# A cross-attention and FFN kernel: row maxima of two banks in one instruction, their transposes first in attention, additions ahead of low parts

## The chip, the cores and the metric

The kernel runs on one core of a Trainium2 chip. The metric is the time of one execution on the device, in microseconds (us), as the median of several runs. Five engines run their own instruction lists in order and meet at semaphores: TensorE (PE, with its weight loads as PEld), VectorE (DVE), ScalarE (ACT), GpSimd (POOL) and SyncE (SP), which issues nearly all DMAs.

## The reference, cut to what matters

```
x   [4, 2048, 512], ctx [4, 154, 512], 16 heads of 32, 8 key/value heads
q1,q2 = split(LN(x) @ Wq.T)   k1,k2 = split(ctx @ Wk.T)   v = ctx @ Wv.T
attn  = (softmax(q1 k1^T) - lam * softmax(q2 k2^T)) v        # per head, 154 keys
x     = x + (rmsnorm(attn) * g * (1 - 0.8 + 0.6 exp(-3.6))) @ Wo.T
h     = gelu(LN(x) @ ternary(w1).T + b1)                     # 2048 wide
x     = x + LN(h) @ ternary(w2).T + b2
```

All in float32. Both softmaxes subtract the maximum of each row of scores.

## The kernel before, in words

The 8192 rows of x are cut into 16 blocks of 512 rows (NBLK), each block into four tiles of 128 (TT). Products are made from float16 parts: a tensor is split into a high part (ScalarE casts or scales) and a low part (VectorE subtracts), and TensorE multiplies high with high, high with low and low with high.

**Row maxima.** For each of the 4 x 32 rows of scores (4 tiles, 32 units: two softmaxes of 16 heads) the maximum is needed before attention. `row_scores` writes the scores of one tile and three units (two in the last group) into a PSUM bank, 462 numbers a partition, and `row_max` on VectorE reduces that bank to three numbers. There are 44 such banks' worth to a block (NT). They are made for block i+1 inside the FFN loop of block i, MAXIMA_AT[j] of them beside step j. From block 2 on they rotate over four banks: PSUM banks 6, 7, 0, 1; blocks 0 and 1 have two. When all are there, `split_maxima` makes float16 parts of the negated maxima (step TLAST of the loop), TensorE transposes them (`transpose_maxima`, token c), VectorE copies the result (`copy_maxima`, last in its loop), and SP stores it as two further rows of the stacked queries by DMA. The first scores of the next attention wait for that DMA.

**Attention** of a block follows the list ATTEND, which every engine walks, each taking the tokens that concern it:
- s0 to s7: TensorE's scores (4 units a time, L1518 and L1523), ScalarE's exponentials and high parts (L807 to L812), VectorE's low parts (L1127).
- v0 to v7: TensorE's product with the values (L1541 to L1548) and VectorE's normalise; at odd numbers also the difference of both softmaxes and the statistics (L1136 to L1150).
- q0 to q3: queries of the next block (L1430 to L1432), ScalarE's q_hi, GpSimd's q_lo.
- t0 to t2: high and low part of a pair of heads (ScalarE, and VectorE L1155), then SP transposes them by DMA into `rows`, for the output projection behind v7. A fourth comes behind the list. SP issues twelve DMAs of the next block's stacked queries behind t0.
- e1 to e3, h1 to h4: what is left of the FFN of the block before: its second product for tile 1 (e), 2 and 3 (h), in steps of hidden groups given by LATE (L1599). Each step is two matmuls.
- g: TensorE's sums of gelu and its square (L1620), VectorE's gelu_norm, on GpSimd the constant's additions (L672) and a power.
- y0 to y3: VectorE's addition of the FFN's product to x_res (`add_ffn`, L1247), which frees the PSUM bank. Scores 1 wait for y0 and y1, the queries q1 for y2, q2 for y3.
- z0 to z3: VectorE's last addition (`add_shift`, L1256), SP's store and the load of x for the next block.

Behind the list come the output projection (pairs 0 to 2 of all tiles, then pair 3; it goes through L1430 to L1432 as well), the second layer norm and the transposes of its rows.

**The FFN loop** has 16 steps (JH): TensorE's first product (`hidden`, L1583), row scores (L1486), the second product for tile 0 of three steps before (`ffn_step`, L1609); ScalarE's gelu, high part and square; VectorE's maxima (L1105) and gelu low part (L1221), and in steps 7 to 10 low parts of x rows (L1098); on GpSimd two running sums a step (L681, L685). `ffn_step` of a step waits for its gelu low part.

Of the kernel before, what the change touches and what calls it, by code (L numbers as in the profile page):

```python
# [24 lines left out]
ALU = mybir.AluOpType  # L25
ACT = mybir.ActivationFunctionType
AX = mybir.AxisListType
# [4 lines left out]
BATCH, T, S = 4, 2048, 154  # L32
H, KV, DH = 16, 8, 32
HID = 2048
JH = HID // P
TB = 512
TT = TB // P
NBLK = BATCH * T // TB
BLK_PER_BATCH = T // TB
UNITS = 2 * H  # L40
# [14 lines left out]
UPB = 3  # L55
TBLK = -(-UNITS // UPB)
NT = TT * TBLK
# [4 lines left out]


ATTEND = [(w[0], int(w[1:] or 0)) for w in (
    "e1 c g e2 s0 e3 y0 y1 q0 s1 h1 v0 z0 z1 s2 h2 v1 y2 s3 q1 t0 z2 v2 s4 h3 v3 s5 h4 t1 y3 v4 s6 q2 z3 v5 s7 t2 q3 v6 v7").split()]


LATE1 = 0
LATE = {("e", 1): (1, LATE1, 10), ("e", 2): (1, 10, 14), ("e", 3): (1, 14, JH),
        ("h", 1): (2, 0, 8), ("h", 2): (2, 8, JH), ("h", 3): (3, 0, 8), ("h", 4): (3, 8, JH)}  # L70


# [24 lines left out]
LOADS_AT = {14: (0,), 15: (1,), 16: (2, 3), 17: (4, 5), 18: (6,), 19: (7,), 20: (8,)}  # L97
SUMS_BY_ACT, SUMS_BY_DVE = {17: 0, 19: 2, 20: 4, 22: 5, JH * 2: 7}, {JH * 2: 1, JH * 2 + 1: 3, JH * 2 + 2: 6, JH * 2 + 3: 8}
VECTORS_AT = (1, 2, 3, 5, 6)
MAXIMA_AT = (1, 2, 2) + (3,) * (JH - 3)  # L100
TLAST = JH - 1
PAIR = 2 * UPT
QDMA = 3 * UPT * 16

# [7 lines left out]
def maxima_beside(j):  # L112

    first = sum(MAXIMA_AT[:j])
    return list(range(first, first + MAXIMA_AT[j]))


def wait(eng, sem, c, per, k):

    if isinstance(c, int) and c * per + k <= 0:  # L120
        return
    eng.wait_ge(sem, c * per + k)
# [10 lines left out]
def build(nc, x, ctx, wq, wk, wv, wo, lam, g, ln1_g, ln1_b, w1, b1, ln2_g, ln2_b, w2, b2, out):  # L133
# [7 lines left out]
    with ExitStack() as es:  # L141
# [3 lines left out]
        def sem(name):  # L145
            return es.enter_context(nc.semaphore(name))

        ps = es.enter_context(nc.psum_tensor("ps", [P, 8, 512], F32))
        B_SREST, B_Q, B_O, B_L = 4, 5, 6, 7

        def row_bank(c, tb):

            return (B_O, B_L, 0, 1)[tb % row_banks(c)]

        def row_banks(c):

            return 2 if c < 2 else 4

        def ffn_bank(tt):

            return (2, 3, B_Q, B_Q)[tt]
# [69 lines left out]
        negmax = probs_raw[:, 6 * TB:6 * TB + TT * UNITS].rearrange("p (t u) -> p t u", t=TT)  # L231
# [3 lines left out]
        def x_split(tt):  # L235
# [99 lines left out]
        s_t, s_tmax, s_nmhi, s_nmlo, s_nmt, s_nmc, s_nmst = (sem(n) for n in (  # L335
            "row_scores", "row_max", "negmax_hi", "negmax_lo", "negmax_transposed", "negmax_copied", "negmax_stacked"))
# [589 lines left out]
        def _(dve):  # L926
# [174 lines left out]
            def row_max(c, tb):  # L1101
                b, tt = divmod(tb, TT)
                u0, u1 = UPB * b, min(UPB * b + UPB, UNITS)
                wait(dve, s_t, c, NT, tb + 1)
                dve.tensor_reduce(negmax[:, tt, u0:u1],  # L1105
                                  ps[:, row_bank(c, tb), 0:(u1 - u0) * S].rearrange("p (u s) -> p u s", s=S),
                                  AX.X, ALU.max, negate=True).then_inc(s_tmax, 1)

            def split_maxima(c):
                wait(dve, s_tmax, c, NT, NT)  # L1110
                wait(dve, s_nmt, c, 1, 0)
                dve.memset(negmax16[:, :, 2:, :], 0.0)
                dve.tensor_scalar(negmax16[:, :, 0, :], negmax, 1.0 / MSCALE, None, ALU.mult).then_inc(s_nmhi, 1)
                wait(dve, s_nmhi, c, 1, 1)
                dve.scalar_tensor_tensor(negmax16[:, :, 1, :], negmax, 1.0 / MSCALE, negmax16[:, :, 0, :],
                                         ALU.mult, ALU.subtract).then_inc(s_nmlo, 1)
# [142 lines left out]
            def iteration(i):  # L1259
                ahead, ahead2 = i < NBLK - 1, i < NBLK - 2  # L1260
                if i == 0:
                    for n in range(ROUNDED_AHEAD):
                        ternary(JH + n)
                for what, n in ATTEND if i else FIRST:
                    if what == "s":
                        probs_lo(i, n)
                    elif what == "v":
                        normalise(i, n)
                    elif what == "t":
                        attn_lo(i, n)  # L1270
                    elif what == "w" and n + ROUNDED_AHEAD < JH:
                        ternary(JH + n + ROUNDED_AHEAD)
                    elif what == "b":
                        bias_vector()
                    elif what == "r":
                        ln1_stats(n)
                        ln1_rows(n)
                    elif what == "x":
                        x_lo(n)
                    elif what == "g" and i:  # L1280
                        gelu_norm(i - 1)
                    elif what == "y" and i:
                        add_ffn(i - 1, n, ffn_bank(n))
                    elif what == "z" and i:
                        add_shift(i - 1, n)
                mid_rows(i, ahead2)
                if ahead2:
                    ln1_stats(i + 2, (2, 3))
                h_lo(i)
                if ahead2:  # L1290
                    ln1_offsets(i + 2)
                for j in range(JH):
                    beside = maxima_beside(j) if ahead else []
                    for tb in beside[:2]:
                        row_max(i + 1, tb)
                    gelu_lo(i, j)
                    if i == 0:
                        output_vectors(j)
                    for tb in beside[2:]:
                        row_max(i + 1, tb)  # L1300
                    if ahead2 and j in X_LO_AT:
                        x_rows_lo(i + 2, X_LO_AT[j])
                    if ahead and j == TLAST:
                        split_maxima(i + 1)
                if ahead:
                    copy_maxima(i + 1)
# [25 lines left out]
        def _(pe):  # L1332
# [139 lines left out]
            def row_scores(c, tb):  # L1472

                b, tt = divmod(tb, TT)
                u0, u1 = UPB * b, min(UPB * b + UPB, UNITS)
                if tb == 0:
                    pe.wait_ge(s_katt, 16 * (c // BLK_PER_BATCH + 1))
                p = (u1 - 1) // PAIR
                if tt == 0 and (b == 0 or p > (u0 - 1) // PAIR):
                    wait_stacked(pe, c, p % 2, p // 2 + 1)  # L1480
                if tb >= row_banks(c):
                    wait(pe, s_tmax, c, NT, tb - row_banks(c) + 1)
                elif tb == 2:
                    wait(pe, s_q32, c, QM, QM)
                for w, u in enumerate(range(u0, u1)):
                    ins = pe.matmul(ps[:, row_bank(c, tb), w * S:(w + 1) * S], stack[0:STK, u, tt * P:(tt + 1) * P],  # L1486
                                    k_att[0:STK, key_unit(u), 0:S], start=True, stop=True)
                ins.then_inc(s_t, 1)
# [135 lines left out]
            def iteration(i):  # L1624
                ahead, ahead2 = i < NBLK - 1, i < NBLK - 2
                for what, n in ATTEND if i else FIRST:
# [7 lines left out]
                    elif what == "v":  # L1634
                        values(i, n)
                    elif (what, n) in LATE and i:
                        tt, j0, j1 = LATE[what, n]
                        ffn_late(i - 1, tt, range(j0, j1))
# [77 lines left out]
```

## Time and profile before

| | us |
|---|---|
| median of three runs | 2522.12 |
| lowest and highest | 2520.97, 2540.89 |
| profiled execution | 2530.05 |
| its span, first to last instruction | 2528.2 |
| granted TensorE clock, mean | 0.938 |

Busy shares are those of the profiled execution. A block's period is the distance between the starts of two FFN tails (L1599 x20) in its trace.

### The profile page before, as it was taken

How to read it: one execution, taken by the hardware profiler on the slowest of the kernel's cores; microseconds unless marked ns; L12 is line 12 of the kernel's file. 1: busy time of each engine (PE TensorE's matmuls, PEld its weight loads, DVE VectorE, ACT ScalarE, POOL GpSimd, SP SyncE). 2: the span in 40 equal slices, each digit the busy share in tenths (PEclk: the TensorE clock that was granted, in tenths of full speed). 3: DMA queues.
4: the chain of work that ended last, by engine and by line, in shares of the span. 5: the costliest groups of instructions: out<-in, count | busy, mean ns of one | idle time of the engine just before them, and what ended most of it. 6: DMA issues, size and time to landing. Idle time of an engine off the chain costs nothing.

```text
span 2528.2 us, 45089 instructions
## 1 busy us (share of the span) xinstructions
PE 2196.8 (87%) x18239; PEld 1200.9 (48%) x18239; DVE 1844.8 (73%) x3030; ACT 1513.4 (60%) x1973; POOL 1032.1 (41%) x803
## 2 busy tenths in 40 slices
PE   7778889898988989898898989889898988989878
PEld 5444355454545445454554545445454544545443
DVE  4776779587787958678786867778686787867663
ACT  3674567565566756556665655666565566655554
POOL 2302607145170714417172451717245170623507
PEclk9878999999999999999999999999999998999989
DMA  7323022121412212131321213122141312212010
GB/s 290 101 52 83 18 81 55 44 76 31 101 37 86 50 44 77 30 84 39 91 59 44 76 31 82 41 81 55 40 94 31 81 43 75 60 34 69 14 39 17
DMA packets 253007, 160.14 MB, mean 63 GB/s; under 512 B 171812, under 2 KB 221580, under 8 KB 252288
## 3 DMA queue, kind: packets, MB, share of 16 engines
q1 hardware_dynamic: 249792, 152.07, 22.4%
q0 software_dynamic: 3008, 5.20, 0.6%
q8 instruction: 144, 2.36, 0.4%
q14 instruction: 63, 0.52, 0.1%
HBM read 51.82 MB, written 20.38 MB: 29 GB/s over the span
## 4 chain that ended last, share of the span: by engine, by line
PE 46%; DVE 34%; ACT 10%; issue 6%; DMA 3%; SPq 1%; POOL 1%; DVEq 0%; POOLq 0%; ACTq 0%
DVE arena L1105 12%; PE ps L1599 10%; DVE arena L1221 10%; PE ps L1430 6%; PE ps L1431 5%; PE ps L1432 5%; PE ps L1583 5%; ACT p L812 3%; PE ps L1518 3%; ACT arena L809 3%; DVE arena L1098 2%; DMA stack_raw<-row_words 2%; ACT arena L807 2%; DVE arena L1247 1%; DVE attn_raw L1141 1%
## 5 line engine op out<-in xcount | busy, mean ns | idle before, releaser
L685 POOL TENSOR_TENSOR attn_raw<-attn_raw 128x512 f32<-128x512 f32 x448 | 643.5, 1455 | 51.8 <-ACT attn_raw L837 22.5
L663 POOL TENSOR_TENSOR q<-q 128x512 f16<-128x512 f32 x128 | 168.0, 1317 | 916.4 <-ACT q L798 915.1
L1583 PE MATMUL ps<-rows,w1T 128*128 128x512 f16 x2048 | 486.9, 381 | 2.2 <-DVE rows L1216 2.2
L1105 DVE TENSOR_REDUCE arena<-ps 128x3 f32<-128x462 f32 (+1 forms) x704 | 401.8, 612 | 32.9 <-PE ps L1486 32.2
L1599 PE MATMUL ps<-w2T,arena 128*128 128x512 f16 x1440 | 361.1, 407 | 0.0
L807 ACT ACTIVATE arena<-ps 128x1024 f32<-128x1024 f32 x128 | 130.9, 1023 | 367.2 <-PE ps L1518 367.2
L1221 DVE SCALAR_TENSOR_TENSOR arena<-attn_raw,vec_cols,arena 128x512 f16<-128x512 f32 x256 | 301.8, 1179 | 51.5 <-ACT arena L835 49.9
L1127 DVE TENSOR_TENSOR p<-arena,p 128x1024 f16<-128x1024 f32 (+1 forms) x128 | 190.9, 1492 | 137.5 <-ACT p L812 128.3
L832 ACT ACTIVATE attn_raw<-ps,vec_cols,wstep 128x512 f32<-128x512 f32 x256 | 197.7, 772 | 153.6 <-PE ps L1583 150.9
L1583 PEld LDWEIGHTS ps<-rows,w1T 128*128 128x128 f16 x2048 | 192.9, 98 | 194.5 <-issue 3.7
L1486 PE MATMUL ps<-k_att,stack_raw 96*128 96x154 f16 x2048 | 228.7, 233 | 47.7 <-DVE arena L1105 45.2
L1127 DVE TENSOR_TENSOR attn_raw<-arena,attn_raw 128x1024 f16<-128x1024 f32 (+1 forms) x128 | 189.2, 1489 | 89.9 <-ACT attn_raw L812 83.1
L1430 PE MATMUL ps<-arena,wqT_hi 128*128 128x512 f16 x512 | 202.0, 394 | 54.4 <-DVE arena L1247 41.6
L1486 PEld LDWEIGHTS ps<-k_att,stack_raw 96*128 96x128 f16 x2048 | 163.5, 98 | 173.2 <-DVE arena L1105 88.0
L1599 PEld LDWEIGHTS ps<-w2T,arena 128*128 128x128 f16 x1440 | 142.9, 104 | 192.2 <-issue 60.1
L796 ACT ACTIVATE q<-ps 128x512 f32<-128x512 f32 x128 | 76.7, 599 | 259.8 <-PE ps L1432 259.7
L1609 PE MATMUL ps<-w2T,arena 128*128 128x512 f16 x608 | 173.1, 380 | 38.8 <-DVE arena L1221 38.8
L1431 PE MATMUL ps<-arena,wqT_hi 128*128 128x512 f16 x512 | 201.7, 394 | 0.0
L1432 PE MATMUL ps<-arena,wqT_lo 128*128 128x512 f16 x512 | 201.2, 393 | 0.0
L1518 PE MATMUL ps<-stack_raw,k_att 99*128 99x512 f16 x512 | 136.9, 391 | 62.9 <-DVE arena L1247 43.6
L835 ACT ACTIVATE arena<-attn_raw,vec_cols 128x512 f16<-128x512 f32 x256 | 184.8, 722 | 8.3
L809 ACT ACTIVATE arena<-ps 128x1536 f32<-128x1536 f32 x128 | 185.1, 1446 | 2.1 <-PE ps L1523 2.0
(191 smaller groups left out, 4520.9 us busy)
## 6 DMA issues: line engine op xcount, KB each, us to landing
stack_raw<-q SPq DMA_DIRECT2D x744, 64.0 KB, 2.0
arena<-in_x SPq DMA_DIRECT2D x64, 256.0 KB, 2.8
out<-arena SPq DMA_DIRECT2D x64, 256.0 KB, 2.0
arena<-in_x SPq DMA_DIRECT2D x14, 1024.0 KB, 5.5
arena<-in_L_ffn_w SPq DMA_DIRECT2D x7, 1024.0 KB, 15.5
rows<-in_x SPq DMA_DIRECT2D x2, 1024.0 KB, 6.9
stack_raw<-in_L_xattn_Wq SPq DMA_DIRECT2D x8, 256.0 KB, 9.8
k_att<-k_store SPq DMA_DIRECT2D x4, 495.0 KB
```

Source lines behind the costliest of these rows:

```text
L685: ins = pool.tensor_tensor(acc[:, e, :], acc[:, e, :], src[:, j % NG, :], ALU.add)
L809: act.activation(probs[:, buf, 2:5, :], ps[:, upper_banks(c, gi), :], ACT.Exp).then_inc(s_p, 1)
L1105: dve.tensor_reduce(negmax[:, tt, u0:u1], ps[:, row_bank(c, tb), 0:(u1 - u0) * S].rearrange("p (u s) -> p u s", s=S), AX.X, ALU.max, negat ...
L1127: ins = dve.tensor_tensor(split[:, 1, slices, :], probs[:, buf, slices, :], split[:, 0, slices, :], ALU.subtract)
L1221: dve.scalar_tensor_tensor(gg16[:, j, 1, :], gelu_t[:, j % NG, :], g2_col[:, j:j + 1], gg16[:, j, 0, :], ALU.mult, ALU.subtract).then_inc( ...
L1430: pe.matmul(dst, w_hi, r_hi, start=first, stop=False)
L1431: pe.matmul(dst, w_hi, r_lo, start=False, stop=False)
L1432: return pe.matmul(dst, w_lo, r_hi, start=False, stop=last)
L1486: ins = pe.matmul(ps[:, row_bank(c, tb), w * S:(w + 1) * S], stack[0:STK, u, tt * P:(tt + 1) * P], k_att[0:STK, key_unit(u), 0:S], start=T ...
L1518: ins = pe.matmul(ps[:, i if i < 2 else upper + i - 2, :], k_att[0:STKM, key_unit(u), 0:P], stack[0:STKM, u, :], start=True, stop=True)
L1583: ins = pe.matmul(ps[:, B_H + j % 2, :], w1T[:, k, j * P:(j + 1) * P], rows16[:, e, k, :], start=(k == 0 and e == 0), stop=(k == KD - 1 an ...
L1599: ins = pe.matmul(ps[:, ffn_bank(tt), :], gg16[:, j, e, tt * P:(tt + 1) * P], w2T[:, j, :], start=(j == 0 and e == 0), stop=(j == JH - 1 a ...
```

## The change

Five things change.
- `row_max_pair` reduces two neighbouring banks (6 and 7, or 0 and 1) in one instruction of 924 elements and gives six maxima. It waits for both banks' scores and counts two on its semaphore. Blocks 0 and 1 keep single ones.
- MAXIMA_AT becomes even: 2, 2, 2, 4, 2, 4, ... and nothing in the last step. `split_maxima` moves to step 14 (TLAST), ahead of the gelu low part of step 15.
- In ATTEND c goes ahead of e1. e1, e2 and e3 (10, 4 and 2 steps) become e1 and e2 (8 and 8), and e2 stands behind s0.
- y0 and y1 go ahead of s0, y2 ahead of v1, y3 ahead of t1. On TensorE h1 goes behind v0.
- z0 and z1 go behind t0, z2 goes beside z3, t2 goes from behind s7 to behind v6.

```
-    "e1 c g e2 s0 e3 y0 y1 q0 s1 h1 v0 z0 z1 s2 h2 v1 y2 s3 q1 t0 z2 v2 s4 h3 v3 s5 h4 t1 y3 v4 s6 q2 z3 v5 s7 t2 q3 v6 v7").split()]
-LATE1 = 0
-LATE = {("e", 1): (1, LATE1, 10), ("e", 2): (1, 10, 14), ("e", 3): (1, 14, JH),
+    "c e1 g y0 y1 s0 e2 q0 s1 v0 h1 s2 h2 y2 v1 s3 q1 t0 z0 z1 v2 s4 h3 v3 s5 h4 y3 t1 v4 s6 q2 z2 z3 v5 s7 q3 v6 t2 v7").split()]
+LATE = {("e", 1): (1, 0, 8), ("e", 2): (1, 8, JH),
         ("h", 1): (2, 0, 8), ("h", 2): (2, 8, JH), ("h", 3): (3, 0, 8), ("h", 4): (3, 8, JH)}
-MAXIMA_AT = (1, 2, 2) + (3,) * (JH - 3)
-TLAST = JH - 1
+MAXIMA_AT = (2, 2, 2, 4, 2, 4, 4, 2, 4, 2, 4, 4, 2, 4, 2, 0)
+TLAST = JH - 2

+            def row_max_pair(c, tb):
+                b, tt = divmod(tb, TT)
+                u0, u1 = UPB * b, min(UPB * b + UPB, UNITS)
+                bank = row_bank(c, tb)
+                wait(dve, s_t, c, NT, tb + 2)
+                dve.tensor_reduce(negmax[:, tt:tt + 2, u0:u1],
+                                  ps[:, bank:bank + 2, 0:(u1 - u0) * S].rearrange("p b (u s) -> p b u s", s=S),
+                                  AX.X, ALU.max, negate=True).then_inc(s_tmax, 2)
+
+            def row_maxima(c, tbs):
+                if c < 2:
+                    for tb in tbs:
+                        row_max(c, tb)
+                else:
+                    for tb in tbs[::2]:
+                        row_max_pair(c, tb)

-                    for tb in beside[:2]:
-                        row_max(i + 1, tb)
+                    row_maxima(i + 1, beside[:2])
                     gelu_lo(i, j)
...
-                    for tb in beside[2:]:
-                        row_max(i + 1, tb)
+                    row_maxima(i + 1, beside[2:])
...
-                    wait(pe, s_tmax, c, NT, tb - row_banks(c) + 1)
+                    wait(pe, s_tmax, c, NT, tb - row_banks(c) + (1 if c < 2 else 2 - tb % 2))
```

## Rows read from the trace of the kernel before

**Rows 1.** The page's head and its first part: busy us, share, instructions.
```profile
span 2528.2 us, 45089 instructions
PE 2196.8 (87%) x18239; PEld 1200.9 (48%) x18239; DVE 1844.8 (73%) x3030; ACT 1513.4 (60%) x1973; POOL 1032.1 (41%) x803
```

**Rows 2.** Waits: who waited for whom, us in total, times, longest.
```profile
PE ps L1518 <- DVE arena L1247: 43.6, 15, 6.2
...
PE ps L1430 <- DVE arena L1247: 41.6, 28, 2.5
...
PE ps L1430 <- ACT arena L809: 11.4, 14, 0.8
```

**Rows 3.** Timeline of TensorE in one block: start, us, instruction, [idle before].
```profile
1183.38 0.60 PE L1609 MATMUL ps<-w2T,arena 128*128 128x512 f16 x2 [2.29 <-DVE arena L1221]
1183.83 6.17 PE L1599 MATMUL ps<-w2T,arena 128*128 128x512 f16 x20
...
1190.05 1.90 PE L1620 MATMUL ps<-ones,attn_raw 128*128 128x1 f32 x16
1191.81 1.89 PE L1599 MATMUL ps<-w2T,arena 128*128 128x512 f16 x8
1194.68 1.04 PE L1518 MATMUL ps<-stack_raw,k_att 99*128 99x512 f16 x4 [0.98 <-DMA stack_raw<-row_words]
...
1203.25 1.02 PE L1518 MATMUL ps<-stack_raw,k_att 99*128 99x512 f16 x4 [2.67 <-DVE arena L1247]
...
1208.00 0.22 PE L1541 MATMUL ps<-v_att,p 128*128 128x132 f16 x1
...
1209.89 1.02 PE L1518 MATMUL ps<-stack_raw,k_att 99*128 99x512 f16 x4
...
1220.37 0.38 PE L1430 MATMUL ps<-arena,wqT_hi 128*128 128x512 f16 x1 [2.47 <-DVE arena L1247]
...
1253.82 0.27 PE L1541 MATMUL ps<-v_att,attn_raw 128*128 128x132 f16 x1 [3.39 <-DVE attn_raw L1141]
```

**Rows 4.** The chain of waits in the FFN loop: start, us, what ended last.
```profile
1146.38 1.64 DVE arena L1105 x3
1148.03 1.26 DVE arena L1221
...
1158.56 1.13 DVE arena L1098
...
1160.78 0.66 DVE arena L1221
```

**Rows 5.** Groups by form, whole span (busy us, mean ns); GpSimd's timeline row.
```profile
L1105 DVE TENSOR_REDUCE arena<-ps 128x3 f32<-128x462 f32 x640 | 374.4, 627 | 31.9 <-PE ps L1486 31.3
...
L672 POOL TENSOR_TENSOR arena<-arena,out_const 128x512 f32<-128x512 f32 x64 | 79.6, 1272 | 0.0
...
L1105 DVE TENSOR_REDUCE arena<-ps 128x2 f32<-128x308 f32 x64 | 27.4, 466 | 1.0 <-PE ps L1486 0.9
...
1143.07 42.60 POOL L685 TENSOR_TENSOR attn_raw<-attn_raw 128x512 f32<-128x512 f32 x28
```

**Rows 6.** Timeline of VectorE in the same block: start, us, instruction.
```profile
1184.57 1.25 DVE L1115 SCALAR_TENSOR_TENSOR arena<-arena 128x128 f16<-128x128 f32 x1
...
1207.20 3.13 DVE L1127 TENSOR_TENSOR attn_raw<-arena,attn_raw 128x1024 f16<-128x1024 f32 x2 [4.10 <-ACT attn_raw L812]
...
1252.09 0.69 DVE L1155 TENSOR_TENSOR attn_raw<-attn_raw 128x512 f16<-128x512 f32 x1
```

**Rows 7.** DMA issues: count, median us from issue to landing.
```profile
rows<-attn_raw SPq DMA_TRANSPOSE x64, 2.7
```

**Rows 8.** Windows of whole blocks: us, busy by engine, granted clock, DMA share, GB/s.
```profile
740.24:884.97 144.73, 128.67 (x1110) 70.59 (x1108) 111.72 (x182) 91.13 (x116) 63.86 (x48) 0.97 0.22 60
...
1034.01:1183.99 149.98, 132.97 (x1109) 71.70 (x1108) 112.41 (x182) 91.03 (x116) 62.98 (x48) 0.94 0.21 58
...
sum 1921.29, PE 1710.34 PEld 927.49 DVE 1447.53 ACT 1179.59 POOL 821.10; mean PE 131.56 PEld 71.35 DVE 111.35 ACT 90.74 POOL 63.16
```

## The prediction

> **What bounds the kernel now.** The page's shares come first: TensorE has work in 87% of the span, VectorE in 73% [rows 1]. A share does not say what ends last, so the waits come next: sums over the whole span of who stood idle for whom [rows 2]. On TensorE they are few and large, and each is one place in a block, repeated. The timeline of one steady block shows the places [rows 3]: 2.29 us before the last FFN step (for VectorE's L1221), 0.98 before the first scores (for the DMA of the maxima), 2.67 before the second scores and 2.47 before the queries q1 (both for L1247, the additions), 3.39 before the last values. The sums of rows 2 give two more, 11.4 / 14 = 0.82 before q0 (for a bank that ScalarE reads) and (41.6 - 14 x 2.47) / 14 = 0.50 before q2. That is 13.1 us of the 144.7 to 150.0 us of a block [rows 8]. Between them TensorE runs without a gap, so in attention it is the bound and each removed gap counts, unless a later gap waits for the same thing.
>
> The FFN loop is different. There the chain of waits is VectorE's alone for 40 us: three maxima, one gelu low part, over and over, 1.64 + 1.26 = 2.90 us a step, and 0.55 + 1.13 + 1.10 + 0.66 = 3.43 us in the four steps with x_rows_lo [rows 4]. GpSimd is as full: 28 sums back to back in 42.60 us [rows 5].
>
> **The additions before the low parts (y0 y1 ahead of s0, y2 ahead of v1).** Nothing is added, only VectorE's order changes. Today y1 stands behind the two low parts of scores 0, which wait for ScalarE's halves, and scores 1 can't start before y1 has emptied its bank: TensorE gets to them only at 1203.25 [rows 3]. After the change y1 waits only for e2 on TensorE. Behind e2 stands q0, 12 x 0.216 = 2.6 us; an addition takes 0.7 us plus about 0.2 to be seen. So the wait is gone with 1.6 us to spare. What the waiting y1 now holds up on VectorE is the low part 0, and values 0 needs that (h1 no longer stands between them). Count from the end of e2: y1 to +0.9, then 2.9 for the low parts to +3.8; TensorE reaches values 0 at +2.6 + 1.28 = +3.9. It just fits; bounds 0 and 0.5 us a block, I take 0. For q1: y2 now comes right behind low part 2 instead of behind v1's normalise, product and statistics (some 2.5 us). Scores start at 1203.25 and their low parts end at 1207.20 + 3.13, 7.05 us later [rows 3, 6]; so, counted from scores 2, low part 2 ends at +7.05 and y2 at +7.75, and TensorE, with 1.28 for scores, 3.45 for h2, 1.89 for values (1208.00 to 1209.89) and 1.28 again, reaches q1 at +7.9. The same count for the old order gives a wait of 2.4, and 2.47 was measured, so the count can be trusted to 0.1. The wait goes to 0.
> The sum: s1's wait was 43.6 us in 15 blocks, of which the last block (no queries to cover y1) keeps 0.9: 42.7. q1's is 14 x 2.47 = 34.6 [rows 2, 3].
> q2's 0.50 goes too, since y3 passes the 0.6 us of t1, but the next wait takes it: values 7 waits for a VectorE chain that starts at scores 6, which TensorE runs before q2. Nothing gained.
>
> **Transposed maxima first, e1 and e2 recut to 8 + 8 steps.** The copy of the maxima and their DMA take from the end of the transposes, where the sums start at 1190.05, to the first scores at 1194.68: 4.63 us [rows 3]. Only the sums (1.75) and 8 matmuls (1.73) lie beside that now. Afterwards it is 16 matmuls (3.45) and the sums: 5.2, enough. The 0.98 goes in 15 blocks: 14.7 us. The 0.82 before q0 goes too: 16 matmuls in place of 4 lie between scores 0 and q0. That is 11.4 us in all [rows 2]. c can only come first if split_maxima is done; that is what the loop's change is for.
>
> **Two banks at a time.** A maximum of 462 elements takes 627 ns, one of 308 takes 466 [rows 5]: 1.045 ns an element. So 924 elements take 1.11 us. Back to back, singles come 0.547 us apart (1.64 for three [rows 4]), 0.08 less than their duration; a pair then costs 1.03 against 1.094. Bounds: 0.95 if all of one fixed part (0.146) is saved, and 1.20 if the pair can't overlap its neighbours and pays a little more. I take 1.03, nearest to the rows. The Trainium skill, "VectorE: DVE Perf Modes", section on the TRN2 errata, gives an instruction that reads PSUM a fixed 120 cycles; as an estimate by that page a pair saves 0.125 us and not 0.066, 1.1 us more a block. The spacing in the trace speaks for the smaller value.
> In the stretch that VectorE bounds (from step 3 to the last gelu low part) stand 35 long and 3 short maxima now: 35 x 0.547 + 3 x 0.39 = 20.3 us. Six of 44 instead of five lie ahead of it afterwards, so 17 long and 2 short pairs: 17 x 1.03 + 2 x 0.71 = 18.9. Saved 1.4. But split_maxima (2.0 us: it follows the last maximum at 1183.8 and its last operation ends at 1185.8 [rows 6]) moves from behind the last gelu low part to ahead of it, because step 14 is now the last with maxima. The last FFN step waits for that low part. Net: the loop ends 0.6 us later, 14 x 0.6 = 8.4, and the first block's loop (two banks, single maxima, no saving) pays the whole 2.0. The split's cover, e1, is thus given away; what is bought with it is the 0.98 + 0.82 above. Steps of four and of two (VectorE 2 x 1.03 + 1.26 = 3.3 and 2.3 us, TensorE with ten matmuls of 0.216 and four or two banks of 0.19 each 2.9 and 2.55) don't average worse, since four banks hold two pairs.
>
> **t2 after v6, z2 beside z3.** This is the part that costs. VectorE's attn_lo for pair 2 (0.6 us) started at 1252.09 [rows 6], its DMA was issued when it ended, and such a transpose lands 2.7 us after issue [rows 7]: 1255.5, a microsecond before the output projection at 1256.5. Now normalise 6 goes first. Values 7 starts when that ends, and at the same moment t2 begins: 0.6 + 0.2 + 2.7 = 3.5 us to landing, with only values 7 (1.9) as cover. The output projection waits 1.6 us, a wait that steady blocks don't have now: 15 x 1.6 = 24 us. Bounds 1 and 2.5 (landing spreads). Values 7's own wait: t2's 0.6 leaves its chain and z2's 0.67 joins it, so +0.07, 1 us in all, and the 3.39 becomes some 4.0. z0 and z1 move behind t0, where v3 has h3 (3.5 us) as cover; on SP the two stores and one load now follow the 8.3 us of stacking, and t1 comes 13 us after t0, so they still fit.
>
> **The clock.** Blocks with the same waits take 144.73 us at a granted clock of 0.97 and 149.98 at 0.94 [rows 8]. The matmuls behind a gap show why: the 20 behind the 2.29 us took 6.17 us [rows 3], where 20 x 0.216 is 4.3; the slow part of them ran at 1.2 GHz instead of 2.4, after TensorE had idled. The thirteen blocks of the sum row have 1921.29 us, 147.8 each, 3.1 more than the best of them. Four places in a block have gaps over 2 us, and two of them vanish: I take half, 1.5 x 14 = 21 us. Bounds: nothing (the fall moves to the gaps that are left, which grow a little), and all, 43 us.
>
> **Sum.** 42.7 + 34.6 + 14.7 + 11.4 = 103.4 of waits; minus 24 (transpose), 8.4 + 2 (loop), 1 (v7): 68. Plus 21 of clock: 89. The profiled execution had 2530.05 (span 2528.2), 8 above the median of the runs: 2441 and 2433.
>
> **Rivals.** *The cheap end* (chance 0.13): the transpose lands in time or behind a v7 that waits anyway, and the whole clock excess is back: 103 - 11 + 43 = 135, less 8 for a wait of 0.5 that stays, gives 2395. For it: gaps fall from seven to four a block.
> *GpSimd paces the loop* (0.12): its sums of 1.27 us when alone take 1.44 in the loop without a gap [rows 5], so it needs 2.88 a step where VectorE would need 2.80 on average. It ends at 1185.67, 2.3 us behind the last gelu low part, so it has fallen behind already. If VectorE's single operation waits for it more often, the 1.4 us saved by pairs is not seen and up to as much again is lost: 14 x 2 = 28, so 2461. The Trainium skill, "SBUF — State Buffer", says of the shared port pair that it is an exclusive lock, held for the whole instruction, against VectorE operations with two SBUF inputs. By that rule a step needs 2 x 1.27 + 0.66 = 3.2, and 2.90 is measured, so the lock isn't full here, though L1221's 1.26 in plain steps against 0.66 in others [rows 4] shows that there is one.
> *The gain moves* (0.08): the counts with a margin of 0.2 (values 0, q1) fail, each by 0.5 to 1 us, and the clock gives nothing: 68 - 21 = 47, so 2475.
> *Slower* (0.03): a reduction over two banks is much dearer than two single ones. It starts only when both banks are full and frees both at once, so what it costs more is paid at once in the loop. The 19 pairs of the bound stretch eat the gain of 89 / 14 = 6.4 us at 1.03 + 6.4 / 19 = 1.37 us a pair; at 1.7 the kernel takes about 2520 + 14 x 19 x 0.33, some 2600. No row shows a reduction over two banks; against it stands that 1.045 ns an element held from 308 to 462.
> *It doesn't do what it says* (0.03): TensorE's order is bound elsewhere, by ScalarE's exponentials. ScalarE idles some 2 us before each scores today, so there is room; then about 2510.
>
> **Chances.** The forecast 0.61, then 0.13, 0.12, 0.08, 0.03, 0.03. Less than 1% (25 us) is about what a measurement can't tell from nothing. Faster by more than 1%: 0.94; within: 0.03; slower: 0.03. The range reaches from the cheap end's neighbourhood (2400) past the case where the gain moves (2475).
>
> **What would show it.** In the profile after: no TensorE wait for L1247 over 0.5 us outside the last block; no wait for the DMA of row_words; a new wait at L1430 for the DMA into rows of some 1.6 us; the wait for L1221 at the end of the loop up from 2.3 to 2.8 us; a pair's duration 1.11 us; values 7 waiting 4.0 us; a mean clock of 0.95. The prediction is wrong if q1 or values 0 waits for low parts, if the loop is longer than 50 us, or if the clock falls.

## The result, and the profile after

The changed kernel takes 2400.51 us (median of four runs, 2400.07 to 2407.51) against 2530.19 (2520.97 to 2540.89): a ratio of 0.949, 95% interval 0.944 to 0.954. The profiled execution has a span of 2399.0 us, 129 less than before. The forecast was 2433 for the kernel, 89 us less for the profiled execution as for the median: right in sign and kind, and too small by 40 us. The result lies at the very edge of the range, whose lower end was 2400; that it lies inside is luck.

The page's head and first part, and the chain that ended last by engine:

```profile
span 2399.0 us, 45089 instructions
PE 2150.0 (90%) x18239; PEld 1188.0 (50%) x18239; DVE 1804.7 (75%) x2722; ACT 1510.4 (63%) x1973; POOL 1047.7 (44%) x803
...
PE 46%; POOL 23%; DVE 13%; ACT 8%; issue 5%; DMA 3%; SPq 1%; POOLq 0%; DVEq 0%; ACTq 0%
```

TensorE runs the same 18239 matmuls and is busy 46.8 us less [rows 1]. The same work in less time is the clock: the clock's own records in the two traces put 246.7 us of TensorE's busy time before at 1.2 GHz and 155.2 after. What runs at 1.2 GHz takes twice as long as at 2.4, so half of the difference, 45.8 us, is what the clock gave back, and that is all but one of the 46.8. The remaining 82.4 us are idle time that went. Hold these two apart, for the experiments below do the same. The last line tells a third thing: GpSimd, 1% of the chain before, is now 23%. A chain names only the work that ended last: in both kernels 28 of GpSimd's sums stand back to back beside the loop, in 42.60 us before [rows 5] and in 43.55 after, so little had to move for the chain to go over to it.

Who waited for whom, TensorE's part (us in total, times, longest). Lines have moved: L1532 is the scores' product, L1263 the additions, L1555 the values, L1237 the gelu low part, L1444 queries and output projection.

```profile
PE ps L1555 <- DVE attn_raw L1157: 90.7, 51, 4.3
...
PE ps L1623 <- DVE arena L1237: 29.7, 15, 2.5
...
PE ps L1500 <- DVE arena L1113: 26.4, 40, 1.1
...
PE ps L1444 <- DMA rows<-attn_raw: 21.8, 17, 7.8
...
PE ps L1500 <- DVE arena L1104: 11.0, 28, 1.2
...
PE ps L1634 <- POOL attn_raw L684: 8.3, 12, 0.7
...
PE ps L1532 <- DMA stack_raw<-row_words: 4.5, 1, 4.5
...
PE ps L1532 <- DVE arena L1263: 0.9, 1, 0.9
```

Against [rows 2]: 43.6 us for the additions before scores 1 have become 0.9, in the last block, where no queries cover them; the 41.6 and 11.4 before queries have no line any more. In their place stand 21.8 us for the transposing DMA (8.2 before) and 20 us more before values.

One block's timeline of TensorE, at the places of [rows 3] (start, us, instruction, idle before it):

```profile
1288.32 1.03 PE L1532 MATMUL ps<-stack_raw,k_att 99*128 99x512 f16 x4
...
1302.96 0.39 PE L1444 MATMUL ps<-arena,wqT_hi 128*128 128x512 f16 x1
...
1331.59 0.22 PE L1555 MATMUL ps<-v_att,p 128*128 128x132 f16 x1 [0.52 <-DVE attn_raw L1157]
...
1337.93 0.22 PE L1555 MATMUL ps<-v_att,attn_raw 128*128 128x132 f16 x1 [4.28 <-DVE attn_raw L1157]
1341.17 0.61 PE L1444 MATMUL ps<-woT_hi,rows 128*128 128x512 f16 x1 [0.59 <-DMA rows<-attn_raw]
...
1411.48 0.61 PE L1623 MATMUL ps<-w2T,arena 128*128 128x512 f16 x2 [1.93 <-DVE arena L1237]
...
1416.46 1.95 PE L1634 MATMUL ps<-ones,attn_raw 128*128 128x1 f32 x16 [0.69 <-POOL attn_raw L684]
```

Scores 1 (first row) and q1 (second) start without a gap. Of seven gaps of 13.1 us, six of 8.3 us are left (the sixth, not in the rows, is 0.32 us ahead of values 3), and half of that is one: 4.28 us before values 7. The loop, counted from its first hidden product to the end of its last FFN step, takes 48.11 us in most blocks, where it took 49.62.

Groups by form (busy us, mean ns), against [rows 5]:

```profile
L1113 DVE TENSOR_REDUCE arena<-ps 128x6 f32<-128x924 f32 x280 | 306.4, 1110 | 28.7 <-PE ps L1500 28.5
...
L1237 DVE SCALAR_TENSOR_TENSOR arena<-attn_raw,vec_cols,arena 128x512 f16<-128x512 f32 x256 | 244.0, 953 | 43.1 <-ACT arena L834 41.8
```

A pair takes 1110 ns, as worked out from the two lengths of single ones. Not forecast: the gelu low part, which the change does not touch, took 1179 ns on average and takes 953.

Whole blocks (us, busy by engine, clock, DMA share, GB/s), against [rows 8]:

```profile
863.14:1000.12 136.98, 126.79 (x1110) 70.07 (x1110) 108.92 (x160) 90.85 (x117) 64.35 (x48) 0.99 0.25 63
1000.12:1142.58 142.46, 131.97 (x1111) 71.71 (x1110) 110.21 (x158) 90.85 (x117) 65.64 (x49) 0.94 0.23 61
```

Blocks still differ, 5.5 us between these two, and 5.2 of that is busy time, so the clock; but the best now has 0.99 and not 0.97. TensorE's work in a block at 2.4 GHz is thus at most 126.8 us, where the best block before had 128.67.

### The profile page after: what moved, and what is told of

It is laid out like the page before. It is cut to its first block, busy times and chain, and to the rows that moved or that the text cites. A ratio compares the mean times of both kernels' runs of the same rounds, so it can differ in the third digit from the quotient of the medians.

```text
span 2399.0 us, 45089 instructions
## 1 busy us (share of the span) xinstructions
PE 2150.0 (90%) x18239; PEld 1188.0 (50%) x18239; DVE 1804.7 (75%) x2722; ACT 1510.4 (63%) x1973; POOL 1047.7 (44%) x803
## 4 chain that ended last, share of the span: by engine, by line
PE 46%; POOL 23%; DVE 13%; ACT 8%; issue 5%; DMA 3%; SPq 1%; POOLq 0%; DVEq 0%; ACTq 0%
POOL attn_raw L684 21%; PE ps L1613 10%; PE ps L1444 5%; PE ps L1445 5%; PE ps L1597 5%; PE ps L1446 5%; DVE attn_raw L1143 3%; PE ps L1532 3%; DVE arena L1272 2%; DMA rows<-attn_raw 2%; ACT arena L808 2%; ACT attn_raw L811 2%; DVE attn_raw L1157 1%; ACT arena L806 1%; POOL attn_raw L680 1%
## 5 line engine op out<-in xcount | busy, mean ns | idle before, releaser
L684 POOL TENSOR_TENSOR attn_raw<-attn_raw 128x512 f32<-128x512 f32 x448 | 658.1, 1488 | 47.9 <-ACT attn_raw L836 18.1
L1113 DVE TENSOR_REDUCE arena<-ps 128x6 f32<-128x924 f32 (+1 forms) x308 | 328.5, 1081 | 30.4 <-PE ps L1500 28.5
L1613 PE MATMUL ps<-w2T,arena 128*128 128x512 f16 x1440 | 338.5, 390 | 0.0
L1237 DVE SCALAR_TENSOR_TENSOR arena<-attn_raw,vec_cols,arena 128x512 f16<-128x512 f32 x256 | 244.0, 953 | 43.1 <-ACT arena L834 41.8
L1143 DVE TENSOR_TENSOR attn_raw<-arena,attn_raw 128x1024 f16<-128x1024 f32 (+1 forms) x128 | 202.5, 1593 | 71.0 <-ACT attn_raw L811 64.1
L1500 PE MATMUL ps<-k_att,stack_raw 96*128 96x154 f16 x2048 | 202.4, 232 | 41.0 <-DVE arena L1113 26.4
L1500 PEld LDWEIGHTS ps<-k_att,stack_raw 96*128 96x128 f16 x2048 | 152.7, 98 | 145.0 <-DVE arena L1113 38.7
L1444 PE MATMUL ps<-arena,wqT_hi 128*128 128x512 f16 x512 | 195.8, 382 | 1.4 <-DVE arena L1091 1.4
L1445 PE MATMUL ps<-arena,wqT_hi 128*128 128x512 f16 x512 | 195.1, 381 | 0.0
L1446 PE MATMUL ps<-arena,wqT_lo 128*128 128x512 f16 x512 | 195.0, 381 | 0.0
L1623 PE MATMUL ps<-w2T,arena 128*128 128x512 f16 x608 | 168.3, 380 | 29.7 <-DVE arena L1237 29.7
L651 POOL TENSOR_TENSOR rstd<-var,neghalf 128x4 f32<-128x4 f32 x48 | 48.6, 1012 | 273.2 <-DVE var L1184 209.8
```

The source lines that it names most:

```text
L684: ins = pool.tensor_tensor(acc[:, e, :], acc[:, e, :], src[:, j % NG, :], ALU.add)
L1113: dve.tensor_reduce(negmax[:, tt:tt + 2, u0:u1], ps[:, bank:bank + 2, 0:(u1 - u0) * S].rearrange("p b (u s) -> p b u s", s=S), AX.X, ALU.m ...
L1143: ins = dve.tensor_tensor(split[:, 1, slices, :], probs[:, buf, slices, :], split[:, 0, slices, :], ALU.subtract)
L1237: dve.scalar_tensor_tensor(gg16[:, j, 1, :], gelu_t[:, j % NG, :], g2_col[:, j:j + 1], gg16[:, j, 0, :], ALU.mult, ALU.subtract).then_inc( ...
L1444: pe.matmul(dst, w_hi, r_hi, start=first, stop=False)
L1445: pe.matmul(dst, w_hi, r_lo, start=False, stop=False)
```

## The experiments

Times are medians. Kernel before, beside these runs: medians of 2524 to 2527 us, single executions from 2512 to 2541. "Idle" and "busy" are TensorE's, from the profiled executions: the kernel before has 331.4 us idle and 2196.8 busy, the changed one 249.0 and 2150.0. A profiled execution is one of several and need not be the median one.

The table has the kernels in which every instruction's work is the same (us); those with filled gaps or cut sums have their numbers further down. "At 1.2 GHz" is the part of the busy time that falls into stretches of the lower clock, by the clock's records in the trace; the last column takes half of it off the busy time, which leaves what it would be at 2.4 GHz throughout.

| kernel | time | idle | busy | at 1.2 GHz | busy, all at 2.4 GHz |
|---|---|---|---|---|---|
| before | 2530.19 | 331.4 | 2196.8 | 246.7 | 2073.5 |
| changed | 2400.51 | 249.0 | 2150.0 | 155.2 | 2072.5 |
| order alone | 2466.47 | 279.9 | 2181.3 | 219.9 | 2071.3 |
| loop alone | 2502.35 | 323.5 | 2190.5 | 236.9 | 2072.0 |
| changed, single maxima | 2408.73 | 249.7 | 2155.5 | 167.3 | 2071.8 |
| additions' order alone | 2413.99 | 260.1 | 2146.2 | 151.9 | 2070.3 |
| changed, additions late | 2482.33 | 288.6 | 2189.3 | 244.2 | 2067.2 |
| changed, t2 early | 2397.48 | 244.2 | 2150.6 | 160.1 | 2070.5 |
| changed, z late | 2415.17 | 251.4 | 2161.9 | 183.4 | 2070.2 |
| changed, z late, t2 early | 2407.27 | 241.7 | 2162.7 | 182.9 | 2071.3 |

The last column stays within 7 us of itself while the busy time moves by 51: in these kernels, whatever changes in TensorE's busy time is the clock.

**Half of the change each: the order alone.**

```
 ATTEND, LATE as changed;  MAXIMA_AT, TLAST = JH - 1 and row_max as before
```

> The new order of attention alone (ATTEND and LATE of the change), with the old loop: single maxima, split_maxima behind the last gelu low part. The transposes of the maxima now stand first and must wait for that split. Theory 'the waits': the gaps for L1247, the maxima's DMA and the bank before q0 are gone as in the changed kernel (103 us), the split's 2.0 us lies bare at the start of each block (28 us), transposing DMA 9 us, clock 15 to 20 us back: 2435 to 2450. Rival 'the loop brought the surplus': the order alone brings only what the forecast gave it, less the split: 2455 to 2470. A TensorE wait of about 2 us for L1115 at L1493 in each block under both.

Measured: 2466.47 us, ratio 0.977 (0.972 to 0.982). Idle 279.9, busy 2181.3.

```profile
PE ps L1541 <- DVE attn_raw L1141: 90.1, 50, 4.3
...
PE ps L1493 <- DVE arena L1115: 27.8, 16, 1.9
...
PE ps L1430 <- DMA rows<-attn_raw: 21.1, 16, 7.8
```

The 27.8 us are the split of the maxima laid bare, as expected (28). The waits that the order removes are all gone here too. But busy fell by only 15.5 us, not by 47: the new gap of 1.9 us stands right behind the 2.29 us at the loop's end, two matmuls between them. The time missed the theory's range (2435 to 2450) and fell into that of the rival, "the loop brought the surplus", though by way of the clock: of the waits both had said the same.

**The loop alone.**

```
 MAXIMA_AT, TLAST, row_max_pair as changed;  ATTEND, LATE as before
```

> The new loop alone (maxima of two banks, even MAXIMA_AT, split in step 14) with the old order of attention. By the forecast's sum it is a loss of 0.6 to 0.8 us a block, about 10 us: 2530 to 2540. Rival 'fewer collisions with GpSimd': the gelu low part takes 0.95 us instead of 1.18 on average as in the changed kernel, which gives back 1.8 us a block: 2505 to 2515. Which of them shows in L1221's mean duration and in the length of the loop (49.3 us before).

Measured: 2502.35 us, ratio 0.991 (0.988 to 0.994). Not the loss of the forecast's sum but a gain of some 23 us (single executions 2488.85 to 2516.32, and the profiled one is among the slowest). L1237 takes 947 ns and the loop 48.11 us instead of 49.62: the rival holds. 23 us alone, 59 for the order alone, 125 together: the two need each other, since the split ahead of step 15 is what lets the transposes stand first without a gap.

**Pairs or the pattern of steps.**

```
-                if c < 2:
+                if c < NBLK:          # single maxima in every block
```

> The changed kernel with single maxima in all blocks; MAXIMA_AT, the split's place and the order stay. Theory 'only the instruction's fixed part': 20 pairs in the stretch that VectorE bounds cost 0.066 us more each, 1.2 to 1.3 us a block: 2417 (2412 to 2422). Rival 'the pair shifts the phase against GpSimd': the low parts' mean goes back towards 1.18 us and the loss is 2 to 4 us a block: 2430 to 2455. If MAXIMA_AT alone removed the collisions, 2400 to 2410.

Measured: 2408.73 us (2402.07 to 2412.53), some 8 us above the changed kernel, which ran at another time; the ranges overlap, so no more than "0 to 12 us" can be said for the two-bank instruction from the times. The traces say more: in most blocks the loop takes 48.45 us with single maxima and 48.11 with pairs, 0.34 a block, so some 5 us in all. L1237 takes 928 ns here. So it is not the pair that spares the low parts but the even MAXIMA_AT with the split in step 14. The profile suggests why the pair's 1.4 us a block is hardly seen: at the end of the loop TensorE now waits for GpSimd (the 0.69 us above), which VectorE can't hurry. No run tests that by itself.

**The order of the additions alone.**

```
-"e1 c g e2 s0 e3 y0 y1 q0 s1 h1 v0 z0 z1 s2 h2 v1 y2 s3 ...
+"e1 c g e2 y0 y1 s0 e3 q0 s1 h1 v0 z0 z1 s2 h2 y2 v1 s3 ...
```

> The kernel before with y0 y1 ahead of s0 and y2 ahead of v1, nothing else. y1 then waits for e3, which TensorE has behind scores 0. Theory 'the waits': both gaps (2.67 and 2.47 us) vanish, 77 us, and none comes in their place; with no clock effect 2446, with all of the clock behind these two gaps 2410 to 2420. Rival 'the gain moves': ScalarE or the low parts are late at values 0 and half of it comes back there: 2480.

Measured: 2413.99 us, ratio 0.957 (0.951 to 0.962): moving three tokens of VectorE's list gives all but some 13 us of the whole change. Idle 260.1, busy 2146.2.

```profile
PE ps L1541 <- DVE attn_raw L1141: 77.2, 24, 4.4
...
PE ps L1430 <- DVE arena L1247: 7.0, 14, 0.5
...
PE ps L1518 <- DVE arena L1247: 0.9, 1, 0.9
```

The waits fell by 77.3 us and 6.7 came back before values: 71 of idle time. The profiled execution is busy 50.6 us less besides. It is the fastest of its four; in the medians the gain is 111 us, which leaves some 40 for the clock. That is the expectation's upper case (2410 to 2420): all of the clock behind these two gaps.

**The additions' order undone in the changed kernel.**

```
-"c e1 g y0 y1 s0 e2 q0 s1 v0 h1 s2 h2 y2 v1 s3 ...
+"c e1 g s0 e2 y0 y1 q0 s1 v0 h1 s2 h2 v1 y2 s3 ...
```

> The changed kernel with only the additions' order undone: y0 y1 behind scores 0 and e2, y2 behind v1. By the same count as in the forecast scores 1 then waits 1.0 us (the 16 matmuls of e2 now cover most of the low part), q1 2.3 to 2.5 us: 3.4 us a block, 49 us, without the clock 2449. Theory 'gaps cost the clock too': 10 to 30 us more, 2460 to 2480. Rival 'the order of additions is only as much as its waits': 2440 to 2452.

Measured: 2482.33 us (2479.68 to 2487.20), 82 above the changed kernel.

```profile
PE ps L1444 <- DVE arena L1263: 34.6, 14, 2.5
...
PE ps L1532 <- DVE arena L1263: 11.6, 8, 3.6
```

45 us of waits are back, and the profiled execution has 39.6 us more idle and 39.3 more busy. The time lies just above the upper end of "gaps cost the clock too" (2460 to 2480) and far from that of the rival. From both sides, then: of what the additions' order is worth, waiting is half to two thirds, and the clock the rest.

**Gaps filled, waits left: the kernel before.**

```
+                        if i and n == 1:            # ahead of scores 1
+                            wait(pe, s_p, i, 2 * QM, 1)
+                            for j in range(10):
+                                pe.matmul(ps[:, 0, :], w2T[:, j, 0:P], w2T[:, j, :], start=True, stop=True)
...
+                        if i and n == QM - 1:       # ahead of values 7, 14 of them
```

> The kernel before with matmuls of no use put into two gaps of TensorE in each block: 10 (2.2 us) behind q0, in the gap of 2.67 us before scores 1, and 14 (3.0 us) behind values 6, in the gap of 3.39 us. They write a bank that nobody reads then. No wait changes. Theory 'TensorE's idling lowers its clock, and that is worth as much as the waits': the matmuls behind run at 2.4 GHz, TensorE's busy time less the added 24 x 0.216 x 15 = 78 us falls by 15 to 35 us from 2197, and the kernel gets as much faster though it does more: 2490 to 2510. Rival 'the clock falls at other places instead': no change, 2515 to 2530. If the filling is in the way of something: slower than 2530.

Measured: 2499.38 us, ratio 0.989 (0.986 to 0.993). A kernel with 360 matmuls more is 27 us faster. Its busy time is 2236.3; less 360 x 0.216 = 77.7 that is 2158.6, 38 below the kernel before. At 1.2 GHz stand 153.0 us of it instead of 246.7. No wait was taken away: 11.2 us are listed before scores 1, and 15 x 2.16 = 32.4 of filling stand in the rest of the 43.6. This is the direct evidence that the gaps lower the clock.

**One gap filled: the changed kernel.**

```
+                        if i and n == QM - 1:       # ahead of values 7
+                            wait(pe, s_p, i, 2 * QM, 2 * QM)
+                            for j in range(14):
+                                pe.matmul(ps[:, 0, :], w2T[:, j, 0:P], w2T[:, j, :], start=True, stop=True)
```

> The changed kernel with 14 matmuls of no use (3.0 us) behind values 6, in the gap of 4.28 us before values 7. Theory 'idling lowers the clock': values 7 (2.65 us in the profile, 2.05 elsewhere) and the output projection (10.86, 10.5 at 2.4 GHz) get faster by 1 us a block: 2383 to 2393. But values 7 no longer covers part of the transposing DMA when it gets faster, so the wait for it grows from 0.6 to about 1.2 and takes half of that back: 2390 is the likeliest. Rival: no effect, 2398 to 2405.

Measured: 2410.80 us (2407.17 to 2416.62), 10 slower than the changed kernel, against every case of the expectation. At the place it went as expected: values 7 took 2.06 us instead of 2.65, and the wait for the transposing DMA grew to 1.19 us.

```profile
1343.65 0.39 PE L1444 MATMUL ps<-woT_hi,rows 128*128 128x512 f16 x1 [1.19 <-DMA rows<-attn_raw]
```

In all that wait is 34.8 us instead of 21.8, 13 more. Busy (2189.8) less the filling (14 x 15 x 0.216 = 45) is 2144.4, only 5.6 better than 2150.0: elsewhere, in the block shown behind scores 0, 16 matmuls took 5.49 us where the changed kernel's block had 3.63. These two numbers are the balance, 6 us slower in the profiled execution. So a filled gap helps where nothing else hangs on it, and low stretches can move.

**GpSimd out of the way.**

```
-  ins = pool.tensor_tensor(acc[:, e, :], acc[:, e, :], src[:, j % NG, :], ALU.add)
+  ins = pool.tensor_tensor(acc[:, e, 0:8], acc[:, e, 0:8], src[:, j % NG, 0:8], ALU.add)
```

8 of 512 columns of each sum are added, so nearly all of the sums of gelu and of its square are left out. The kernel before:

> The kernel before, with GpSimd's running sums of steps 2 to 15 over 8 of 512 columns only, so that the sums of gelu and of its square leave out nearly all. Theory 'GpSimd holds up VectorE's operations on two SBUF inputs': L1221 falls from 1.18 to 0.74 us on average, L1098 from 1.20 to 0.73, VectorE's loop shortens by 11 x 0.6 + 4 x 0.5 = 8 us, of which TensorE's own 2.75 us a step leave 3 to 5 us a block: 2460 to 2480. Rival 'the longer low part has another cause': no change, 2515 to 2530.

and the changed one:

> The changed kernel with the same cut of GpSimd's sums (the sums of gelu and its square leave out nearly all). If GpSimd still holds up VectorE here, L1237 falls from 0.95 to 0.74 us and the wait of 0.69 us for GpSimd before the sums goes: 2 to 4 us a block, 2345 to 2370. Rival 'the changed loop is bound by TensorE and VectorE's maxima already': only the 0.69 us goes, 2388 to 2395.

Measured: 2424.89 us (ratio 0.961, 0.957 to 0.964) and 2334.06 us (0.924, 0.921 to 0.928 against the kernel before). In the first:

```profile
L1105 DVE TENSOR_REDUCE arena<-ps 128x3 f32<-128x462 f32 x640 | 378.6, 630 | 37.7 <-PE ps L1486 34.6
...
L1221 DVE SCALAR_TENSOR_TENSOR arena<-attn_raw,vec_cols,arena 128x512 f16<-128x512 f32 x256 | 203.3, 794 | 82.1 <-ACT arena L835 80.3
...
L1098 DVE TENSOR_TENSOR arena<-arena 128x512 f16<-128x512 f32 x56 | 38.0, 678 | 0.0
```

The two VectorE operations with two tensors in SBUF fall from 1179 to 794 ns and from 1205 to 678; the maxima, which read PSUM, stay at 630. So the GpSimd sums cost the kernel before 102 us and the changed one 66, both more than I had expected. In the kernel before this comes through VectorE: TensorE's waits for its maxima and low parts (L1105, L1221) fall from 84.0 to 19.7 us, the loop from 49.6 to 44.2 a block, and 43.6 us of busy time come back with them. In the changed kernel a part is GpSimd itself, since the wait of 8.3 us for it before the sums goes too.

**The new costs taken back: t2 early, z late.**

```
 after_t2_early:  ... v5 s7 t2 q3 v6 v7
 after_z_late:    ... s6 q2 v5 s7 q3 v6 t2 z2 z3 v7
 both:            ... s6 q2 v5 s7 t2 q3 v6 z2 z3 v7
```

> The changed kernel with t2 back ahead of q3, as before the change. The wait for the transposing DMA (0.6 us in most blocks, 13.6 us more than before in all) goes, and values 7 waits up to 0.6 us longer, as the low part of attention is back in its chain. On a balance 0 to 13 us: 2388 to 2401, 2396 likeliest. The forecast had priced the late t2 at 24 us; if that were so, 2385.

Measured: 2397.48 us (2396.39 to 2398.63). The wait for the DMA is back at 8.2 us and values wait 8.5 more: even on the profile but for 5 us, and 3 us in the medians of different sessions. It is the fastest version of all, by less than these runs can settle.

> The changed kernel with z2 and z3 (the last additions of tiles 2 and 3, 2.3 us on VectorE in its profile) moved from ahead of normalise 5 to behind t2. Values 7 waits 4.28 us for a VectorE chain in which they stand. Theory 'that chain sets values 7': its wait falls by the 2.3 us, less up to 0.9 if the low part 7 then waits for ScalarE: 1.4 to 2.3 us a block, 2370 to 2382, with a better clock 2365. Rival 'paid elsewhere': the stores and the load behind them come late on SP, and the second layer norm waits for x_res: 2395 to 2410.

Measured: 2415.17 us (2404.01 to 2419.87). Values wait 38 us less, as the theory said, and it is slower all the same; the rival was right in kind, at another transfer than it named and by more (its range ended at 2410). SP's queue in one block:

```profile
1343.58 1.23 SPq L540 DMA_TRANSPOSE rows<-attn_raw  x1
1344.86 0.58 SPq L551 DMA_DIRECT2D out<-arena  x1
1345.48 0.43 SPq L511 DMA_DIRECT2D arena<-in_x  x1
1345.96 2.00 SPq L551 DMA_DIRECT2D out<-arena  x1
1349.08 1.58 SPq L511 DMA_DIRECT2D arena<-in_x  x2
1350.77 0.38 SPq L500 DMA_DIRECT2D arena<-in_x  x1
1351.20 1.41 SPq L540 DMA_TRANSPOSE rows<-attn_raw  x1
```

The stores of z2 and z3 and the loads that wait for them lie between the third transposing DMA and the fourth, which goes out at 1351.20 and not behind the low part, at 1349.1. The waits at L1444 for these transposes total 62.2 us (21.8 in the changed kernel): 40 more, and the 38 that values saved are gone. Idle time is thus nearly as it was (251.4 against 249.0), and what makes the kernel slower is the clock: 11.9 us more of busy time.

> Both of the two edits before. If they add up: the better of both less 0 to 10 us, 2360 to 2380. With z2 and z3 out of the chain, t2's 0.6 us may fall into VectorE's wait for ScalarE and cost nothing.

Measured: 2407.27 us (2401.85 to 2418.34), between the two and far from the 2360 to 2380 expected: they do not add up. The wait at L1444 is 43.8 us: the fourth transposing DMA's part stays.

## Why the prediction was right, and where its sizes were off

**The additions** were right place by place: scores 1, q1 (counted with a margin of 0.15 us) and values 0 (0.1) start without a gap, and the last block keeps the 0.9 us that the forecast left it. 77.3 us were forecast for these two waits and 77.3 went. q2's 7 us moved to values 7, as said. The maxima's DMA and the bank before q0 gave 14.8 and 11.4, as said.

**The late t2** costs 13.6 us and not 24: values 7 ran at a low clock, 2.65 us instead of 1.9, and so covered more of the DMA. With that gap filled it took 2.06, and the wait rose by 13 us, to about what was forecast. That t2's place matters little is shown by its return.

**Values 7** came out at the price forecast, and the price of what stands before it was missed. Forecast were 0.07 us a block and the 0.50 that moves there from q2, 8 us in all. The gap of 3.39 us in [rows 3] is of one of two kinds: of the 14 blocks before, nine have 3.39 and five have 4.35. After the change all 14 have 4.28, so the sum grew by 7.6 us. Comparing the one block shown with one block after gives 0.89 a block, 0.35 us a block too much.

The two kinds before differ in which of two engines is held up. VectorE's low part for t2 and GpSimd's low part of the queries, both with two inputs in SBUF, run side by side (the first row is from the block of [rows 3], the others from one of the other kind):

```profile
1251.52 2.27 POOL L663 TENSOR_TENSOR q<-q 128x512 f16<-128x512 f32 x1 [5.28 <-ACT q L798]
...
1104.90 1.67 POOL L663 TENSOR_TENSOR q<-q 128x512 f16<-128x512 f32 x1 [5.27 <-ACT q L798]
...
1105.48 1.64 DVE L1155 TENSOR_TENSOR attn_raw<-attn_raw 128x512 f16<-128x512 f32 x1
...
1108.16 0.27 PE L1541 MATMUL ps<-v_att,attn_raw 128*128 128x132 f16 x1 [4.35 <-DVE attn_raw L1141]
```

In the nine blocks with 3.39 us GpSimd's takes 2.27 and VectorE's, at 1252.09 [rows 6], 0.69; in the five with 4.35 us they take 1.67 and 1.64. In the changed kernel t2 has left that place and low part 7 is there instead: 3.83 us instead of 2.88, in every block. The other term was priced rightly: z2 and z3 take 2.31 us together where z3 alone took 1.65, 0.66 more, and 0.67 was put.

What the forecast left out are gaps before other values: 0.52 us before values 6, which wait for the normalise behind z2 and z3, and 0.32 before values 3. That is 12 us in 14 blocks. The first is gone with z late (its trace has no gap there), the second with the additions late; the forecast had looked at z2 and z3 for values 7 alone. That the price of values 7 itself fits is thus partly luck: the 0.95 us by which low part 7 is stretched was not foreseen, nor was the wait of 0.52 shortly before, and by the count of the rows, not by a run of its own, the second takes up most of the first.

**The loop** was forecast 0.6 us longer and is 1.5 shorter; the wait for its last low part fell from 2.29 to 1.93 us where 2.8 was forecast. Counted in waits, the forecast took 10 us off for the loop, and TensorE's waits in and right behind it fell by 9. No wait for GpSimd was forecast there, and 0.69 us a block came. The arithmetic of the pairs held (1110 ns each), and the split does stand ahead of the last low part. What failed is the 1.26 that the forecast carried over for each low part (steps of "2 x 1.03 + 1.26", which "don't average worse"): that duration belongs to one phase against GpSimd. In steady steps of 2.90 us the low part met GpSimd's sum in the same phase each time, 1.26 from its start to the next; in uneven steps it often does not, and many take 0.74 to 1.1. The loop alone and the kernel with single maxima show it in the mean of all (947 and 928 ns, against 1179). GpSimd pays for a part of that: 28 of its sums take 43.55 us instead of 42.60. Its rate was misread as well: the forecast had 1.44 us a sum, but [rows 5] has 28 in 42.60 us, which is 1.52 and so 3.04 a step, as much as VectorE's steps take on average. It was level with VectorE already. I had GpSimd as a rival with a loss; it is both, a gain by the phase, and now a bound of its own, 23% of the chain.

**The clock** is the term that was mis-sized most: 21 us forecast, 43 as its bound, 46.8 measured. The bound was wrong because it took the best block (144.73 us) as free of low clock; its own row had 0.97 and 128.67 us busy, and 126.8 is possible. Rows 8 could have told that. Nor had the two blocks compared there "the same waits": the one of 144.73 us has the gap of 3.39 before values 7 and the one of 149.98 that of 4.35, so 4.3 of the 5.25 us between them are busy time and 0.95 is a wait.

**Sum.** Idle 82.4 against 68, busy 46.8 against 21. In the idle time errors of both signs partly cancel: the late t2 cost 10 us less than forecast and the loop 19 less, the gaps before values 12 more. That the sum of waits came out within 15 us although the loop alone was 19 off is therefore in part luck; the additions' 77.3 is not, and it is what the forecast rests on. The rivals: the cheap end (2395) is nearest to the result, by the clock rather than by the DMA. Pairs dearer than 1.37 us, and a gain that moves on, did not come.

## What to carry to other kernels

Walk every engine's list for an operation that frees a bank or buffer for the busiest engine but stands behind one that nobody needs yet: here two such swaps on VectorE gave 110 of the 125 us. Price a gap of TensorE at more than its length, since the matmuls behind it run slower, and read the cost of the clock from TensorE's busy time for the same instructions rather than from the best block. Look at one place in all blocks before pricing it: the gap before values 7 had two lengths, and the block read had the shorter one. And before moving a token, list what it issues on other queues: z2 and z3 left VectorE's chain and blocked SP's.

## What the runs showed of the hardware

- TensorE's busy time for the same 18239 matmuls was 2146 to 2197 us in ten kernels that differ in order and waits, and 2067 to 2074 in all of them once half of the time at 1.2 GHz is taken off. Adding 360 matmuls in gaps of 2.7 and 3.4 us made the kernel before 27 us faster. The Trainium skill, "TensorE: Matmul & The Clock Gate", section on the HAM clock gate, says that the throttled state is the default and activity releases it. The filled gaps agree: with them 153.0 us of busy time stood at 1.2 GHz instead of 246.7. The clock's records here have the two levels 1.2 and 2.4 GHz and no other.
- One reduction over two PSUM banks costs its elements once and a fixed part once: 462, 616, 924 elements took 633, 795 and 1110 ns.
- GpSimd's additions lengthen VectorE operations on two SBUF tensors by up to 1.1 us and leave PSUM reductions alone. "SBUF — State Buffer" of the Trainium skill says the same of which operations contend, and that the one that starts first holds the shared ports for its whole instruction. The pairs of low parts above agree with that: 2.27 beside 0.69 us, or 1.67 beside 1.64. For a plain step of the loop an estimate by that rule is 3.2 us, and 2.90 was measured; why it is less there stays open.
